# A Macaron block on one core: squarings of a matrix exponential against gates of three chunks moved among the expert tiles

## The chip, the cores and the metric

One core of one Trainium2 chip runs one launch. Times are device microseconds; of the kernel before there are three timed runs and one profiled execution. Five engines run side by side, each with a queue of its own that it works off in order: PE (TensorE), DVE (VectorE), ACT (ScalarE), POOL (GpSimd) and SP (SyncE, which only issues DMA here). They meet by semaphores. PEld is PE's weight load.

## The reference

`x` is 8 sequences of 512 rows of 128 floats. Three steps follow, each on a layer norm of what is there and each with a residual: half of a feed-forward, attention with 16 heads and a linear bias, half of a feed-forward again, with the same weights.

```python
xn = layernorm(x) * gamma + beta
abel_out = gelu(xn @ abel_w + abel_b)
logits = xn @ moe_gate_w + moe_gate_b
topw, topi = top_k(logits, 2)                 # of 8 experts
h = gelu(xn @ ew1[e] + eb1[e]);  eo = h @ ew2[e] + eb2[e]
moe_out = sum over the two experts of softmax(topw) * eo
for i in range(3): moe_out = moe_out @ expm(gens[i])
g = sigmoid(concat(abel_out, moe_out) @ gc_w + gc_b)
out = x + abel_out * (1 - g) + moe_out * g
```

## The kernel before, in words

Eight chunks (one sequence of 512 rows each) stay in SBUF as `x_all`. A feed-forward layer takes two steps.

**Gate of a chunk.** DVE takes statistics for two chunks at a time (`first_statistics`, lines 1414 to 1427), POOL the roots (`first_roots_`, L835), DVE a shift (`gate_shift`, L1628), ACT writes the normalised chunk twice (`z_`, L1140), PE turns it (`transpose_z`, L2197), ACT evacuates it (`xn_`, L1154), PE multiplies (`abel_logits`, L2213), ACT takes the Gelu (`abel_bias`, L1160), DVE finds the two best experts (`gate_top`), PE counts ranks (`ranks`), ACT takes the tanh of the gap, DVE works out the place of each row (`gate_place`, up to L1685), and POOL sends the rows with eight indirect DMAs of 128 rows to DRAM tensors `z_rows`, sorted by expert (`send_z`, L868).

**Expert tiles.** The sorted rows are worked off as 80 tiles of 128 rows: 20 quads of four tiles, 40 pairs of two. There are two runs: quads 0 to 5 (pairs 0 to 11) hold the rows of chunks 0 and 1 (`SPLIT[0] = 2`), quads 6 to 19 (pairs 12 to 39) those of chunks 2 to 7. Each run needs a table of its tiles (`count_rows`, `make_table`), zeros in the gaps between experts (`zero_gaps` on SP) and all its rows in DRAM (`rows_ready`). For each quad SP reads four registers and issues four loads (`load_x`, L715), PE turns them (`x_turn`, L2246), ACT evacuates. For each pair PE does `up` (L2271), ACT the Gelu (L1254), PE `down` (L2286, L2288), DVE the weighting (L1799); DVE also copies the experts' first weights (L1846). SP stores each quad's result in `y_rows` (`store_y`, L683). After the store of the last quad of a run POOL gathers the pairs of a chunk (`gather`, L885) and adds them into x (`sum_pairs`, `finish_x`, L895 to L908); then attention of that chunk can begin (`attention_stats`, L1408, in the first layer beside pair 22 for chunk 0 and 29 for chunk 1).

**The exponential.** The three 128 x 128 generators are scaled by their norms, put through a Taylor series of degree 11 (`transposed_generators`, `second_power`, `third_power`, three times `horner_step`) and squared 18 times. A round squares three matrices: PE computes square and transpose of each (`square`, L2125 and L2126), DVE copies them where the norm asks for it (`keep_squares`, L1555). The product is folded into the experts' second weights (`fold_rotation`), which the first expert tile needs, together with their transposes (`transpose_w2`, evacuated by ACT in `w2_out`).

**The order before** is written out by hand for each engine. Chunks 0 and 1 are gated ahead of the exponential's series; then six turns, for chunks 2 to 7, of one gate and three rounds of squarings; then `fold_rotation`; then the experts. PE's program of the turns is (from line 2331):

```python
for n in range(2, CH):
    if n + 1 < CH:
        transpose_z(n + 1)
    square(range(3 * n - 6, 3 * n - 5))
    ranks(n)
    square(range(3 * n - 5, 3 * n - 4))
    if n + 1 < CH:
        abel_logits(n + 1)
    square(range(3 * n - 4, 3 * n - 3))
    if n - 2 < E // 2:
        transpose_w2(n - 2)
```

DVE's and ACT's follow the same turns, POOL's is `send_z` for chunk after chunk with the roots between. SP's queue holds the stores of the Abel part (`keep_abel`), the copies of key rows for attention (`key_rows`, 512 KB for two heads), the zeros and the loads of x, in one order.

## Time and profile before

| | |
|---|---|
| timed runs | 789.38, 791.55, 793.94 us; median 791.55 |
| profiled execution, first to last instruction | 883.8 us (no other time is given for it) |
| instructions | 16149 |
| PE busy | 683.1 us, 77% of the span |
| DVE busy | 568.2 us, 64% |
| POOL busy | 485.6 us, 55% |
| ACT busy | 410.8 us, 46% |
| first expert tile of the first layer on PE | 149.06 us |

The profiled execution is 92 us longer than the median of the timed runs. Rows give a start and a duration in us from the first instruction; in brackets stands how long the engine was idle before, and what released it. "remote", "issue" and "another core or an unknown queue" are waits without a releaser in the trace. A matmul in fp32 shows as two records; PEclk is the granted clock as a share of 2.4 GHz.

### The profile page before, as it was taken

Reading aid. Unit: us, or ns where it says so; the run is one execution under the profiler, and the core shown is the slowest. Engines: PE = TensorE matmul, PEld = TensorE weight load, DVE = VectorE, ACT = ScalarE, POOL = GpSimd, SP = SyncE. Lnnn points to the kernel's source line nnn. Section 1 sums busy time; section 2 is a strip of 40 time slices with the busy share of each in tenths; the row PEclk is TensorE's granted clock in tenths of the full one; section 3 lists DMA queues with packets and bytes.
Section 4 is the critical chain, followed back from the end, with each engine's and each line's share of the span. In section 5 each row is a group of like instructions: output and inputs, shape, how many; then the busy total and the mean of one; then the engine's idle time right before and its main releaser. Section 6 shows DMA issues by size and latency. Waiting matters only on the chain.

```text
span 883.8 us, 16149 instructions
## 1 busy us (share of the span) xinstructions
PE 683.1 (77%) x4719; PEld 492.3 (56%) x4719; DVE 568.2 (64%) x1922; ACT 410.8 (46%) x931; POOL 485.6 (55%) x588
## 2 busy tenths in 40 slices
PE   1465667979897798997988979999997777838760
PEld 1355656979793354654646545455544466837750
DVE  3675545968767876876767767787673235745538
ACT  2243411545560265664545645556554655615530
POOL 2656554034512666576866768373645466566661
PEclk9968777988898899998999999999997999969985
DMA  8614544744348313023050240302201235233525
GB/s 242 205 48 117 132 123 115 183 112 105 94 113 192 110 31 98 18 65 87 2 130 21 49 103 1 98 17 55 61 13 53 85 78 167 75 93 84 175 96 154
DMA packets 89825, 84.04 MB, mean 95 GB/s; under 512 B 14561, under 2 KB 72556, under 8 KB 89580
## 3 DMA queue, kind: packets, MB, share of 16 engines
q1 hardware_dynamic: 74472, 57.51, 25.8%
q0 software_dynamic: 8800, 19.72, 7.5%
q10 hardware_dynamic: 6468, 5.79, 2.8%
q8 instruction: 40, 0.66, 0.3%
q14 instruction: 45, 0.37, 0.1%
HBM read 43.84 MB, written 31.13 MB: 85 GB/s over the span
## 4 chain that ended last, share of the span: by engine, by line
PE 46%; DVE 15%; another core or an unknown queue 11%; issue 7%; ACT 7%; SPq 5%; ACTq 3%; DMA 3%; POOL 1%; DVEq 0%; POOLq 0%
PE bank L2361 6%; PE bank L2271 6%; PE bank L2401 6%; PE bank L2286 6%; PE bank L2426 6%; SPq L595 4%; DVE mx_of L1923 3%; PE pair L2449 2%; PE bank L2363 2%; ACT beside_parts L1254 2%; DMA qT<-mT_zero 2%; PE pair L2213 2%; PE bank L2246 1%; ACT arena L1326 1%
## 5 line engine op out<-in xcount | busy, mean ns | idle before, releaser
L1326 ACT ACTIVATE arena<-bank 128x512 f32<-128x512 f32 x320 | 184.0, 599 | 175.2 <-PE bank L2401 147.1
L1923 DVE TENSOR_REDUCE mx_of<-bank 128x4 f32<-128x512 f32 x320 | 204.2, 684 | 81.9 <-PE bank L2361 42.9
L2401 PE MATMUL bank<-qT,kZ 128*128 128x512 f32 (+3 forms) x512 | 156.9, 377 | 19.2 <-ACT arena L1326 12.4
L975 POOL TENSOR_SCALAR_AFFINE_SELECT arena<-arena 128x256 f32<-128x256 f32 (+1 forms) x192 | 95.4, 521 | 123.9 <-ACT arena L1326 122.5
L2361 PE MATMUL bank<-kZ,qT 128*128 128x512 f32 x320 | 148.5, 481 | 15.7 <-DVE mx_of L1923 6.2
L2401 PEld LDWEIGHTS bank<-qT,kZ 128*128 128x128 f32 x512 | 95.7, 197 | 49.2 <-ACT arena L1326 24.1
L868 POOL DMA_INDIRECT z_rows<-beside_kZ,place x80 | 78.7, 984 | 51.5 <-DVE place L1685 29.8
L2361 PEld LDWEIGHTS bank<-kZ,qT 128*128 128x128 f32 x320 | 63.1, 200 | 70.7 <-issue 31.4
L885 POOL DMA_INDIRECT sums<-y_rows,y_place x56 | 54.4, 971 | 84.9 <-DMA y_rows<-arena 70.0
L2426 PE MATMUL bank<-arena,vA 128*9 128x512 f32 (+3 forms) x1024 | 92.4, 440 | 5.2 <-POOL arena L975 2.7
L1254 ACT ACTIVATE beside_parts<-bank,hidden_bias 128x128 f32<-128x128 f32 x160 | 45.5, 381 | 69.6 <-remote 44.0
L2286 PE MATMUL bank<-w_rot,beside_parts 128*128 x320 | 51.2, 297 | 31.7 <-ACT beside_parts L1254 29.0
L1254 ACT ACTIVATE arena<-bank,hidden_bias 128x128 f32<-128x128 f32 x160 | 45.5, 371 | 48.7 <-PE bank L2271 33.4
L1799 DVE TENSOR_SCALAR arena<-bank,arena 128x132 f32<-128x132 f32 x128 | 39.3, 348 | 44.3 <-remote 25.1
L944 POOL DMA_INDIRECT y_rows<-arena x48 | 49.3, 1026 | 31.8 <-DVE arena L1799 20.5
L2286 PEld LDWEIGHTS bank<-w_rot,beside_parts 128*128 128x128 f32 x320 | 43.9, 197 | 36.2 <-issue 35.3
L2286 PE MATMUL bank<-w_rot,arena 128*128 x320 | 50.4, 295 | 7.0 <-issue 5.2
L868 POOL DMA_INDIRECT z_rows<-w,place x48 | 47.0, 979 | 13.4 <-issue 13.4
L2271 PE MATMUL bank<-beside_parts,beside_qT 128*128 128x128 f32 x320 | 46.6, 286 | 8.3 <-issue 5.1
L2363 PE MATMUL bank<-fixed,ident_bf 128*128 128x512 bf16 x128 | 52.5, 410 | 0.0
L2271 PE MATMUL bank<-arena 128*128 128x128 f32 x320 | 47.0, 291 | 3.8 <-DVE arena L1846 2.2
L2286 PEld LDWEIGHTS bank<-w_rot,arena 128*128 128x128 f32 x320 | 44.6, 200 | 9.0 <-issue 8.2
(286 smaller groups left out, 1306.7 us busy)
## 6 DMA issues: line engine op xcount, KB each, us to landing
arena<-z_rows SPq DMA_DIRECT2D x128, 66.0 KB
qT<-parts SPq DMA_DIRECT2D x42, 128.0 KB
kZ<-parts SPq DMA_DIRECT2D x168, 32.0 KB
y_rows<-arena SPq DMA_DIRECT2D x20, 264.0 KB, 3.3
kZ<-bias_k_r SPq DMA_DIRECT2D x8, 512.0 KB
beside_kZ<-y_rows SPq DMA_DIRECT2D x7, 528.0 KB, 3.9
z_rows<-in_spare SPq DMA_DIRECT2D x4, 528.0 KB
z_rows<-in_spare SPq DMA_DIRECT2D x32, 66.0 KB
```

Of the source, the lines that this page charges most:

```text
L868: g_.indirect_dma_start(z_rows[run], bass.IndirectOffsetOnAxis(place[g % DEEP][:, k, t:t + 1], 0), zz(g)[:, k, t, :], None).then_inc(z_sen ...
L885: g_.indirect_dma_start(terms(0, c)[0][:, t, k, :], None, y_rows[run], bass.IndirectOffsetOnAxis(y_place[:, c, k, t:t + 1], 0)).then_inc(s ...
L975: g_.affine_select(out=cut, in_=cut, compare_op=ALU.is_ge, fill=0.0, base=0, pattern=[[0, 2], [0, blocks], [1, P]], channel_multiplier=-1) ...
L1254: a_(hidden_rows(layer, p)[:, i, j, :], ps_up[p % 2][:, P * n:P * (n + 1)], ACT.Gelu, bias=hidden_bias[:, j, bass.ds(e, 1)]).then_inc(hidd ...
L1326: a_(dst, src, ACT.Exp).then_inc(exp_ok.sem, 1)
L1923: v.tensor_reduce(mx_of[:, queries, :, t, keys], ps_a[n % NA][:, :].rearrange("p (q n) -> p q n", q=NQ), AX.X, ALU.max).then_inc(reduced.s ...
L2271: last = mm(into, tile(w1_e, j), tile(turned_x(layer, q), t), start=True, stop=True)
L2286: mm(into, hidden_rows(layer, p)[:, i, j, :], w2_rot[:, bass.ds(e, 1), j, :].rearrange("p a n -> p (a n)"), start=(j == 0), stop=False)
L2361: last = mm(into, qT[u][:, t, P * queries:P * (queries + 1)], heads, start=True, stop=(queries != keys))
L2363: last = mm(into, ident_bf[:, :], mask_qk[:, :].unsqueeze(1).to_broadcast([P, NQ, P]), start=False, stop=True)
L2401: return mm(outp, kZ[u][:, h, lo:lo + P], qT[u][:, t, lo:SEQ], start=start, stop=True, skip_group_check=(kind != "full"))
L2426: last = mm(ps_o[32 * q:32 * q + HD + 1, kb * P:SEQ], vA[u][:, kb, NG * q + t, :], pT[t % 2][:, q, PT_KB[kb]:PT_KB[kb] + n], start=(kb == ...
```

## The change

The exponential's series goes first on PE and DVE, with the gates of chunks 0 and 1 between its steps. Three turns (chunks 2 to 4) carry six rounds each. The gates of chunks 5 to 7 go among expert pairs 0 to 8, with other PSUM banks; x then has one bank instead of two in the first layer. The second run's table is made at pairs 8 and 9, its first x is turned at pair 12 after `down(11)`. The statistics of chunks 4 to 7 go into the first and third turn. POOL sends in halves around the roots. SP's queue is put in a new order, with the loads of the second run's first five quads in one block after `store_y(4)`. Nine small loads go from ACT's queue to SP's, and ACT starts with a Gelu on four columns of ones. `gather(1)` is split around the sums of chunk 0. Attention's steps beside the experts come one pair later, the bias loads of `load_bias` at pairs 8 and 9 instead of 4 and 6.

```diff
+ROTATED = tuple((3 * q, 3) for q in range(4)) + ((12, 2), (14, 2))
+GATED_FIRST = 5
+ROUNDS = 6
+AT_GAPS, AT_SECOND_RUN = 3, 4
...
+        def ps_x(layer, q):
+            return banks[2 + q % 2] if layer else banks[2]
...
         def ps_z(g):
-            return banks[4][:, :] if g < CH else banks[6]
+            return banks[4] if g <= GATED_FIRST else banks[3] if g < CH else banks[6]
...
+        def turns_at(layer, p):
+            if layer == 0 and p == second_run(layer) - 1:
+                return SWITCH[0]
+            q = p // 2 + 1
+            return q if (p or layer == 0) and p % 2 == 0 and q < QUADS and q != run_start(layer) else None
...
@@ SP @@
-            for g in range(1, 3):
-                keep_abel(g)
+            keep_abel(1)
             zero_gaps(0)
+            keep_abel(2)
             for g in range(2):
                 key_rows_of(g)
...
+            keep_abel(3)
             for q in range(X_TOP):
                 load_x(0, q)
...
+            keep_abel(4)
+            key_rows_of(2)
             sp.wait_ge(w2T_pe, 4)
             for q in range(X_TOP, X_BUFS):
                 load_x(0, q)
-            for g in range(5, CH - 1):
-                key_rows_of(g)
-            key_rows(sp, 0, 2 * (CH - 1), 2)
-            zero_gaps(1)
-            z_sent_up_to(sp, CH - 1)
-            key_rows(sp, 1, 0, NG)
-            for q in range(X_BUFS, QUADS):
-                store_y(q - X_BUFS)
-                load_x(0, q)
+            for q in range(QUADS - X_BUFS):
+                if GATED_FIRST + q < CH:
+                    keep_abel(GATED_FIRST + q)
+                if q == AT_GAPS:
+                    zero_gaps(1)
+                store_y(q)
+                if 1 <= q <= 3:
+                    key_rows_of(q + 2)
+                if X_BUFS + q < SWITCH[0] or q > AT_SECOND_RUN:
+                    load_x(0, X_BUFS + q)
+                if q == AT_SECOND_RUN:
+                    for n in range(max(X_BUFS, SWITCH[0]), X_BUFS + q + 1):
+                        load_x(0, n)
+                if q == AT_SECOND_RUN + 1:
+                    key_rows_of(CH - 2)
+                    key_rows(sp, 0, 2 * (CH - 1), 2)
+                    key_rows(sp, 1, 0, NG)
@@ POOL @@
             send_z(0)
+            send_z(1, (0,))
             first_roots_(2)
-            send_z(1)
+            send_z(1, (1,))
+            send_z(2)
+            send_z(3, (0,))
             first_roots_(3)
-            for g in range(2, CH):
+            send_z(3, (1,))
+            for g in range(4, CH):
                 send_z(g)
@@ ACT @@
+            act.wait_ge(v_ones, 2)
+            a_(th[:, :], vA[1][:, 0, 0:NT, HD], ACT.Gelu)
...
+                    if p == 0:
+                        abel_bias(GATED_FIRST)
+                        z_(CH - 1)
+                        tanh_gap(GATED_FIRST)
+                    if p == 1:
+                        xn_(GATED_FIRST + 1)
+                    if p == 3:
+                        abel_bias(GATED_FIRST + 1)
+                        tanh_gap(GATED_FIRST + 1)
...
-            for n in range(2, CH):
+            for n in range(2, GATED_FIRST):
                 abel_bias(n)
-                if n + 1 < CH:
-                    xn_(n + 1)
+                xn_(n + 1)
                 tanh_gap(n)
-                if n + 2 < CH:
-                    z_(n + 2)
-                if n - 2 < E // 2:
-                    w2_out(n - 2)
+                z_(n + 2)
+                for q in (2 * n - 4, 2 * n - 3):
+                    if q < E // 2:
+                        w2_out(q)
@@ DVE, the turns @@
+            for n in range(2, GATED_FIRST):
+                first = ROUNDS * (n - 2)
                 gate_logits(n)
                 gate_top(n)
+                keep_squares(range(first, first + 1))
                 gate_place(n)
...
+                keep_squares(range(first + 1, first + 2))
                 if n == 2:
+                    first_statistics(2)
+                if n == 3:
+                    make_table(0, TABLE_STAGES[0:1])
+                if n == 4:
+                    first_statistics(3)
+                    gate_shift(6)
+                    gate_shift(7)
+                keep_squares(range(first + 2, first + 3))
...
+                keep_squares(range(first + 3, first + 4))
+                if n == 2:
+                    gate_shift(4)
+                    gate_shift(5)
...
+                keep_squares(range(first + 4, first + 6))
@@ DVE, beside the experts @@
-                    if p == 1:
+                    for g in range(GATED_FIRST, CH):
+                        if p == 3 * (g - GATED_FIRST):
+                            gate_logits(g)
+                            gate_top(g)
+                        if p == 3 * (g - GATED_FIRST) + 2:
+                            gate_place(g)
+                    if p == 8:
                         count_rows(1)
-                        make_table(1)
+                        make_table(1, TABLE_STAGES[0:1])
+                    if p == 9:
+                        make_table(1, TABLE_STAGES[1:3])
@@ PE, experts @@
                 for p in range(PAIRS + 1):
+                    if p == second_run(layer):
+                        down(p - 1)
+                        x_turn(p // 2)
                     if p < PAIRS:
                         up(p)
@@ PE, the prologue @@
             turn_norms()
+            spread_norms()
+            transposed_generators()
             transpose_z(0)
+            second_power()
...
+            third_power()
             transpose_z(1)
+            horner_step(0)
             ranks(0)
             abel_logits(1)
+            horner_step(1)
+            horner_step(2)
             ranks(1)
             transpose_z(2)
             turn_exponential()
...
+            for n in range(2, GATED_FIRST):
+                first = ROUNDS * (n - 2)
+                transpose_z(n + 1)
+                square(range(first, first + 1))
                 ranks(n)
+                square(range(first + 1, first + 3))
+                abel_logits(n + 1)
+                square(range(first + 3, first + 4))
+                for q in (2 * n - 4, 2 * n - 3):
+                    if q < E // 2:
+                        transpose_w2(q)
+                if n == 4:
+                    transpose_b2()
+                square(range(first + 4, first + 6))
             fold_rotation()
@@ PE, beside the experts @@
+                    for g in range(GATED_FIRST, CH):
+                        first = 3 * (g - GATED_FIRST) + 1
+                        if p == first:
+                            ranks(g)
+                        if g + 1 < CH and p == first - 1:
+                            transpose_z(g + 1)
+                        if g + 1 < CH and p == first + 1:
+                            abel_logits(g + 1)
```

## Rows read from the trace of the kernel before

**Rows 1.** The page: span, and the chain by engine
```profile
span 883.8 us, 16149 instructions
...
PE 46%; DVE 15%; another core or an unknown queue 11%; issue 7%; ACT 7%; SPq 5%; ACTq 3%; DMA 3%; POOL 1%; DVEq 0%; POOLq 0%
```

**Rows 2.** Stages: busy us (instructions) of PE, PEld, DVE, ACT, POOL; PEclk, DMA, GB/s
```profile
61.00:139.00 78.00, 50.67 (x360) 46.63 (x358) 42.37 (x227) 23.02 (x54) 41.77 (x43) 0.76 0.49 120
149.10:179.20 30.10, 28.71 (x234) 27.27 (x235) 25.25 (x106) 18.12 (x54) 0.00 (x0) 0.94 0.63 144
179.20:214.80 35.60, 29.98 (x239) 29.12 (x237) 25.40 (x93) 17.52 (x55) 13.90 (x14) 0.86 0.46 108
```

**Rows 3.** The chain, 60 to 150 us, then pieces: start, us, what
```profile
by line: another core or an unknown queue 22.9%; issue 9.7%; DVE arena L1555 8.4%; PE bank L2126 8.1%; PE bank L2125 8.0%; PE bank L2143 5.6%; PE pair L2213 5.1%; DVE top_i L1648 3.6%; ACT beside_kZ L1140 3.5%; DVE top L1645 2.1%; DVE w_rot
...
110.28 8.41 another core or an unknown queue
...
192.40 5.21 issue
```

**Rows 4.** Timeline of the prologue: start, us, engine, operation [idle before <-releaser]
```profile
15.92 1.28 ACT L1140 ACT_TABLE_LOAD   x1 [11.86 <-issue]
...
24.37 0.16 DVE L1478 COPY arena<-bank 128x3 f32<-128x3 f32 x1 [9.78 <-PE bank L2082]
...
47.20 0.22 DVE L1628 SCALAR_TENSOR_TENSOR shift<-mv_g,rstd_g 128x4 f32<-128x4 f32 x2
...
61.02 0.39 PE L2125 MATMUL bank<-arena 128*128 128x128 f32 x2
```

**Rows 5.** The same: z of one chunk on ACT
```profile
65.31 3.19 ACT L1140 ACTIVATE beside_kZ<-x_all,shift,rstd_g 128x128 f32<-128x128 f32 x8 [2.72 <-DVE shift L1628]
```

**Rows 6.** The same: squaring on PE, two matrices at each clock
```profile
98.44 0.39 PE L2125 MATMUL bank<-arena 128*128 128x128 f32 x2
...
98.89 0.39 PE L2125 MATMUL bank<-arena 128*128 128x128 f32 x2
...
136.46 0.63 PE L2125 MATMUL bank<-arena 128*128 128x128 f32 x2
...
137.31 0.64 PE L2125 MATMUL bank<-arena 128*128 128x128 f32 x2
```

**Rows 7.** The same: one chunk's gate on DVE, first, squares between, last
```profile
60.79 0.19 DVE L1633 COPY logit<-pair 128x32 f32<-128x32 f32 x1 [2.38 <-PE pair L2214]
...
63.03 1.10 DVE L1555 COPY_PREDICATED arena<-arena,bank 128x256 f32<-128x256 uint32 x3
...
65.04 0.17 DVE L1685 CAST place<-place_of 128x8 int32<-128x8 f32 x1
```

**Rows 8.** The same, POOL: a scatter, then gathers and sums of chunk 0
```profile
140.43 0.97 POOL L868 DMA_INDIRECT z_rows<-beside_kZ,place  x1 [0.30 <-issue]
...
186.24 1.06 POOL L885 DMA_INDIRECT sums<-y_rows,y_place  x1 [38.07 <-DMA y_rows<-arena]
187.61 0.97 POOL L885 DMA_INDIRECT sums<-y_rows,y_place  x1 [0.30 <-issue]
...
197.91 1.30 POOL L895 TENSOR_TENSOR sums<-sums 128x528 f32<-128x528 f32 x1 [1.75 <-DMA sums<-y_rows,y_place]
...
211.41 0.19 POOL L903 TENSOR_SCALAR gate<-gate 128x4 f32<-128x4 f32 x1 [10.49 <-ACT gate L1181]
```

**Rows 9.** SP's queue: a store, four loads; the page: stores, last column landing
```profile
182.53 0.38 SPq L683 DMA_DIRECT2D y_rows<-arena  x1
183.42 1.88 SPq L715 DMA_DIRECT2D arena<-z_rows  x4
...
y_rows<-arena SPq DMA_DIRECT2D x20, 264.0 KB, 3.3
```

**Rows 10.** Timeline of DVE at the first attention statistics
```profile
214.79 0.87 DVE L1408 BATCH_NORM_STATS2 stat<-x_all 128x6 f32<-128x128 f32 x4 [1.16 <-POOL x_all L908]
```

More of the change, by code:

```diff
@@ L641, in _ @@
                 spare_rows(run)
+            with nc.allow_non_contiguous_dma("the first biases, one to a partition"):
+                for j in range(NJ):
+                    sp.dma_start(hidden_bias[:, j, :], eb1[:, P * j:P * (j + 1)].rearrange("e p -> p e")).then_inc(ld_bias, 16)
             def keep_abel(g):
@@ L918, in first_experts @@
             def first_experts():
-                for b in range(2):
-                    gather(b)
-                    if b:
-                        attention_roots(0)
-                    sum_pairs(0, b)
-                    finish_x(0, b)
+                gather(0)
+                gather(1, (0,))
+                sum_pairs(0, 0)
+                finish_x(0, 0)
+                gather(1, (1,))
+                attention_roots(0)
+                sum_pairs(0, 1)
+                finish_x(0, 1)
                 attention_roots(1)
@@ L1106, in _ @@
             act.dma_start(x_all[:, 2 * NT:, :], xv[:, 2 * NT:, :]).then_inc(ld_x[1], 16)
-            with nc.allow_non_contiguous_dma("the first biases, one to a partition"):
-                for j in range(NJ):
-                    act.dma_start(hidden_bias[:, j, :], eb1[:, P * j:P * (j + 1)].rearrange("e p -> p e")).then_inc(ld_bias, 16)
-            for dst, vec in ((C_QB, q_b), (C_KB, k_b)):
-                act.dma_start(cols[:, dst:dst + 1], vec.rearrange("(p a) -> p a", a=1)).then_inc(ld_w, 16)
-            act.dma_start(cols[:, C_GCB:C_GCB + 1], gc_b.partition_broadcast(P)).then_inc(ld_w, 16)
-            for dst, vec in ((R_VB, v_b), (R_OB, o_b), (R_G1, gc_w[0:D, 0]), (R_G2, gc_w[D:2 * D, 0])):
-                act.dma_start(rows[:, dst:dst + D], vec.partition_broadcast(P)).then_inc(ld_w, 16)
+            act.wait_ge(v_ones, 2)
+            a_(th[:, :], vA[1][:, 0, 0:NT, HD], ACT.Gelu)
             def keep_small():
@@ L2136, in fold_rotation @@
                 mm(banks[3][:, 2 * P:2 * P + ROW], b2_T, rot_x, start=True, stop=True).then_inc(rot_pe, 1)
[L2137 to L2139 removed]
+                for q, (first, n) in enumerate(ROTATED):
                     if q == 3:
                         pe.wait_ge(bias_parts, 1)
[L2142 to L2143 removed]
+                    if q == 4:
+                        wait(pe, xn_ok, GATED_FIRST)
+                        wait(pe, placed, GATED_FIRST - 1, 5)
+                    for i in range(first, first + n):
+                        last = mm(banks[q][:, ROW * (i - first):ROW * (i - first + 1)], w2_T[:, i // NJ, i % NJ, :], rot_x,
                                   start=True, stop=True)
@@ L2204, in abel_logits @@
                     wait(pe, abel_biased, g - 1)
+                    if g > GATED_FIRST:
+                        wait(pe, placed, g - 1, 5)
                 elif g >= CH:
@@ L2218, in ranks @@
                 wait(pe, routed, g)
-                if g < CH:
-                    if g:
-                        wait(pe, placed, g - 1, 5)
-                else:
+                if 0 < g < GATED_FIRST:
+                    wait(pe, placed, g - 1, 5)
+                elif g >= GATED_FIRST:
                     wait(pe, abel_biased, g)
```

155 lines of the change are left out of this document (72 added, 83 removed).

## The prediction

> **What bounds the kernel now.** I read the page first, for its span and its chain [rows 1]: 883.8 us, with 11% of the chain (97 us) put down to "another core or an unknown queue". There is one core, so these are waits for which the trace has no releaser. The timed runs have a median of 791.55 us, 92.25 us less than this span, and about as much as those waits. So I take most of them to belong to the profiled execution, and work every sum twice: as profiled, and with the unknown waits out.
>
> Next, the table by stage [rows 2]. It has the squarings (61 to 139) and the stretches from the first expert tile (149.1, called E below) to pair 12 (179.2) and on to the first attention statistics (214.8). PE is busy 51 of 78 us in the squarings, at a granted clock of 0.76, and 29 of 30 us in pairs 0 to 11. The prologue is a chain of small steps handed between DVE and PE; the experts are bound by PE, some 2.3 us a pair. Everything behind the experts is untouched, so the question is when the first expert stage ends.
>
> The chain [rows 3] gives the unknown waits: 22.9% of the 90 us from 60 to 150, 20.6 us, the longest 8.41 us; in the expert stage PE has one of 5.21 us in the middle of a pair, and there are more.
>
> **Up to the squarings: 11 us less as profiled, 8.6 without unknown waits.** Today DVE stands 9.78 us for the transpose that spreads the norms, because PE has it behind the first chunk's logits, and these wait for an ACT whose first activation comes at 15.92, behind its DMA issues [rows 4]. With the exponential first and nine small loads moved to SP's queue, this idle time goes. The two loads of hidden biases sit behind SP's weights and are needed only at E, the seven others 35 us later than they land; I cost them at nothing. The Gelu put first moves one table load of 1.28 us, like the one in that row, under the wait for statistics. One block of statistics (2.7 us) leaves the stretch too; three Horner steps (6.3 us) enter it. The shift of chunk 2 comes at 47.2 - 9.8 - 2.7 - 2.4 (the unknown wait at 40.7, [rows 3]) + 6.3 + 1 for new hand-overs = 39.6. Two chunks of z on ACT follow at 3.19 each [rows 5], then 0.8 for xn, 2.7 for logits and 0.6 for a transpose: first squaring near 50 against 61.
>
> **The squarings: 2 us less, 8.7 with unknown waits.** All 18 rounds of three matrices stay. On PE a matrix takes 0.45 us at 2.4 GHz and 0.85 at 1.2 GHz [rows 6], a round 1.35 or 2.55. Now: 78 - 20.6 = 57.4 us, less 3.5 for a table is 53.9, or 9.0 for each of six cycles of one gate and three rounds. A gate takes DVE 60.79 to 65.21, less 0.9 for copies of squares inside, so 3.5 us [rows 7]; rounds at 1.8 (the clock is mixed) fill the rest. After: three gates 10.8, 18 rounds 32.4, table 2.5 (a part hides beside rounds), and two statistics moved in, each 2.7 less the 1.35 of a round beside it: 2.7. Three waits are new. In the first cycle PE's second transpose of w2 needs ACT's copy of the first, which sits behind z of chunk 4, whose shift DVE gives only after the fourth round: 3.2 + 0.6 + 0.5 = 4.3 us in which all squaring stands. The same pair of transposes costs 0.7 a cycle later. In the last cycle DVE waits for POOL's roots between statistics and shift: 1.9. Sum 55.3, so 2.1 less than 57.4. Of 20.6 us of unknown waits I keep 14, as a quarter of the instructions leaves and four of eight 512 KB key loads move out. Folding, 10 us, stays. E comes 10.7 us sooner without unknown waits, 19.7 as profiled.
>
> **The start of the second run: 19 us later against E.** The tiles of pair 12 on hold rows of chunks 2 to 7, so they need chunk 7's rows in DRAM. Today these are out before E. After, chunk 5 is placed in pair 2, chunk 6 in 5, chunk 7 in 8. Pair 2 begins at E + 6.4 today; abel, z of chunk 7 and its tanh go between ACT's first pairs, 4 us, so chunk 5 is placed near E + 10. Each chunk is 8 scatters on POOL at 0.97 + 0.30 us [rows 8]; 24 take 30.5, longer than the 20 us between placements, so POOL is the bound: E + 40.5. Landing takes 1.75, by the wait behind the last gather. SP then reads registers and issues four loads (0.9 + 1.9 us, [rows 9]), and they land in some 2.3: E + 47.4. Transpose and evacuation follow: pair 12 at E + 49 against E + 30.2. Both gated steps on PE (2.4 us a chunk) and DVE's 3.5 fit into those 49. PE idles some 12 us, and as ACT and DVE have no other pair, nothing covers it.
>
> One rule speaks further against this. These scatters now run beside DVE's copies of w1, as the gathers of this stage do already: those take 0.97 us, the scatters of the prologue 0.97 too [rows 8]. The Trainium skill (SBUF — State Buffer, "SBUF: two separate sides") says that GpSimd cannot write descriptors while VectorE runs a two-port copy, such as an fp32 copy within SBUF. By the rule the 24 scatters would be longer still; the rows show no such thing.
>
> **The first attention statistics.** They wait for POOL's gathers of chunk 0, which wait for the store of quad 5 (today's first gather starts at 186.2, 38 us idle before it [rows 8]). SP now has that store behind five groups of loads that wait for chunk 7: E + 42.3 + 5 x 2.8 = 56.3, landed after 3.3 [rows 9] at 59.6. Then 8 gathers and 4 of chunk 1 (15.1), 1.75 landing, 3.0 for sums, 3.4 to finish (211.41 to 214.79): E + 82.9. Today DVE gets there at 214.79, E + 65.7 [rows 10]; the step comes one pair later now, which gives 2.1 back: 15 us more as profiled. But today's number holds unknown waits. Without them, gathers and sums end at 200.9 and the finish at 204.4, E + 55.3: then the loss is 25.5.
>
> **What costs nothing.** One PSUM bank for x instead of two: each transpose has two pairs of time. The stores of abel and the key rows in SP's loop wait for work already done when their turn comes, and load_bias is due only at the end. Attention's steps one pair later end inside the stage. If the late key rows (2.5 MB) ran up to the operands, they would cost 1 to 3 us.
>
> **Sum.** As profiled: -19.7 + 15 = -4.7. Without unknown waits: -10.7 + 25.5 = +14.8. If the 92.25 us of difference are all of the 97 unknown us, the timed runs keep one in twenty: +14. If they are shared with the chain's 7% of "issue" (62 us), four in ten are kept: +7. I take the middle, +10: 791.55 + 10 = 801.5 us, with a changed profile near 880, which would look like a small gain. Anything within 0.5% (4 us) is no difference that timing this kernel can tell.
>
> **Rivals.**
> **Faster.** The mechanism is the waits in the squarings: if they are in the timed runs as in the profile, each of the three turns moved out takes its 4 us with it (20.6 us over six cycles is 3.4 each), and the wait at pair 12 falls together with the 5.21 us that stood at 192.4. Then -19.7 + 15, and down to -8 if rounds go at 1.35 us because PE idles less: 783 to 788. It decides once E is more than 20 us sooner in timed runs. For it: waits of up to 8.41 us stand in this stretch. Against: 92 us have to go somewhere. 0.16.
> **No difference.** E gains 16 to 20 and the stage loses as much, or the chunk-5 placement comes at E + 7 and the store of quad 5 is not last: 788 to 795. 0.19.
> **Much slower.** PE comes back from 12 us idle, and from the stop before the statistics, at 1.2 GHz: the window with the stop at 192.4 has a mean clock of 0.86, the one before it 0.94. If scatters of chunk 4 are late too (POOL waits for the roots of chunks 6 and 7 with half of chunk 3 unsent), POOL's 30.8 us begin later by up to 10: 812 to 822. 0.08. The Trainium skill (TensorE: Matmul & The Clock Gate, "What's actually happening") has the clock halved by default and released by activity, which is this cost; the trace agrees.
> **The change does not do what it says:** the squarings end where they do now (139) because 18 rounds are the chain whatever stands between; E gains only the 11 us before them. The result is then the forecast's upper side, 805 to 812, and is held within it.
>
> **Chances.** The forecast, 795.5 to 812, has 0.57. Leaving out some 0.1 below and above gives 785 to 815. Bounds of single terms: the first gains 7 to 12, the squarings -6 to +14 in gain, pair 12 loses 14 to 23 (placement between E + 6 and E + 13), the statistics 10 to 27. Faster 0.16, same 0.19, slower 0.65.
>
> **What would show it.** First squaring near 50; a stop of about 4 us in the first cycle, all engines but ACT idle, ACT in z of chunk 4; first expert tile near 130; POOL in unbroken scatters from E + 10 to E + 40.5; PE idle over 10 us before pair 12, released by the loads from z_rows; DVE idle at the statistics in pair 23, released by POOL's x_all. I am wrong if pair 12 begins before E + 40, or if E is before 120.

## Result and the profile after

The changed kernel takes 806.82 us (median of 4, 803.48 to 809.98), the kernel before beside it 790.46 us (median of 4, 787.67 to 793.94): ratio 1.0207, 95% interval 1.0164 to 1.0250, so slower by 16.4 us. The prediction had 801.5 us, 785 to 815, and slower as the likeliest case.

The profile of before on which the prediction was built spans 883.8 us [rows 1]. The same kernel was profiled once more, unchanged. First lines of the page and the chain by engine, the second execution of the kernel before:

```profile
span 791.0 us, 16149 instructions
...
PE 49%; DVE 20%; DMA 7%; issue 7%; POOL 5%; ACT 4%; ACTq 3%; SPq 3%; DVEq 0%; POOLq 0%
```

and of the changed kernel:

```profile
span 807.5 us, 16155 instructions
...
PE 38%; DVE 20%; issue 11%; POOL 10%; DMA 9%; ACT 5%; SPq 4%; ACTq 1%; DVEq 0%; POOLq 0%
```

The entry "another core or an unknown queue" (11% in [rows 1]) is in neither. What has grown is POOL's share of the chain, from 5 to 10%, and "issue", from 7 to 11%; PE's has fallen from 49 to 38%, with the same 656 us of busy time. From here on "before" is this second execution, and the two spans differ by 16.5 us, which is the timed difference.

E is the first transpose of an expert tile. The marks of before: first squaring, E, pair 12, first attention statistics, first score matmul:

```profile
58.92 0.64 PE L2125 MATMUL bank<-arena 128*128 128x128 f32 x2
...
117.87 1.09 PE L2246 MATMUL bank<-ident,arena 128*128 128x128 f32 x8 [0.69 <-DVEq L1403]
...
147.23 1.00 PE L2271 MATMUL bank<-arena 128*128 128x128 f32 x7
...
174.84 0.86 DVE L1408 BATCH_NORM_STATS2 stat<-x_all 128x6 f32<-128x128 f32 x4
...
226.36 0.71 PE L2361 MATMUL bank<-kZ,qT 128*128 128x512 f32 x2 [0.80 <-DVE arena L1799]
```

The same marks of the changed kernel, with the transpose ahead of pair 12:

```profile
51.37 0.63 PE L2206 MATMUL bank<-arena 128*128 128x128 f32 x2
...
110.33 0.63 PE L2332 MATMUL bank<-ident,arena 128*128 128x128 f32 x4 [1.30 <-DVEq L1448]
...
160.32 0.90 PE L2332 MATMUL bank<-ident,arena 128*128 128x128 f32 x3 [9.06 <-DMA arena<-z_rows]
162.31 2.08 PE L2357 MATMUL bank<-arena 128*128 128x128 f32 x8 [0.87 <-ACT arena L1281]
...
196.07 0.87 DVE L1453 BATCH_NORM_STATS2 stat<-x_all 128x6 f32<-128x128 f32 x4 [2.28 <-POOL x_all L942]
...
243.67 0.73 PE L2450 MATMUL bank<-kZ,qT 128*128 128x512 f32 x2 [1.03 <-DMA kZ<-oT]
```

Subtracting gives the account; "predicted" is the column of the prediction's sum without unknown waits:

| | before | after | difference | predicted |
|---|---|---|---|---|
| start to first squaring | 58.9 | 51.4 | -7.5 | -8.6 |
| first squaring to E | 58.95 | 58.96 | 0.0 | -2.1 |
| E to pair 12 | 29.4 | 52.0 | +22.6 | +18.8 |
| E to first statistics | 57.0 | 85.7 | +28.7 | +27.6 |
| E to first score matmul | 108.5 | 133.3 | +24.8 | +25.5 |
| score matmul to the end | 564.6 | 563.8 | -0.8 | 0 |

The sum is -7.5 + 0 + 24.8 - 0.8 = +16.5.

The stage by windows, before (E to pair 12); columns as in [rows 2]:

```profile
117.90:147.20 29.30, 27.22 (x234) 25.92 (x235) 25.45 (x106) 17.98 (x54) 8.02 (x6) 1.00 0.84 193
```

and after, with the stop ahead of pair 12 as a row of its own:

```profile
110.30:151.30 41.00, 32.73 (x296) 30.73 (x296) 32.24 (x171) 23.74 (x70) 25.00 (x26) 1.00 0.55 142
151.30:162.30 11.00, 1.12 (x4) 0.72 (x4) 2.35 (x14) 0.78 (x1) 2.93 (x1) 0.55 0.48 117
```

Twelve pairs take 41 us instead of 29, with gates between them (PE busy 32.7 us of 41, 27.2 of 29), and then hardly any engine works for 11 us (PE 1.1 us of them, POOL 2.9). What ends the stop, POOL and SP of the changed kernel:

```profile
120.07 1.01 POOL L902 DMA_INDIRECT z_rows<-beside_kZ,place  x1 [8.97 <-DVE place L1738]
...
150.31 0.97 POOL L902 DMA_INDIRECT z_rows<-beside_kZ,place  x1 [0.30 <-issue]
...
148.45 0.50 SPq L629 DMA_DIRECT2D kZ<-bias_k_r  x1
149.71 0.36 SPq L713 DMA_DIRECT2D y_rows<-arena  x1
156.90 11.84 SPq L745 DMA_DIRECT2D arena<-z_rows  x20
168.79 0.42 SPq L713 DMA_DIRECT2D y_rows<-arena  x1
```

Chunk 5's first scatter is at E + 9.7, the last of the 24 at E + 40.0, with its end at E + 41.0. The first row of SP is a load of key rows, 512 KB. SP issues its first load 5.6 us after that scatter's end; its waits in this stretch name the landing of the scatters:

```profile
SPq L535 <- DMA z_rows<-beside_kZ,place: 6.0, 1, 6.0
```

In the squarings the two new stops stand where the prediction put them:

```profile
65.28 1.11 PE L2193 MATMUL bank<-ident,arena 128*128 128x128 f32 x4 [3.85 <-ACT arena L1156]
...
96.25 0.49 PE L2206 MATMUL bank<-arena 128*128 128x128 f32 x2 [2.71 <-DVE arena L1609]
```

The first is the second transpose of w2 behind z of chunk 4. The second is PE waiting for squares while DVE waits for POOL's roots.

### The profile page after: what moved, and what is told of

Same layout as the page of the kernel before. It is cut to its first block, busy times and chain, and to the rows that moved or that the text cites. A ratio compares the mean times of both kernels' runs of the same rounds, so it can differ in the third digit from the quotient of the medians.

```text
span 807.5 us, 16155 instructions
## 1 busy us (share of the span) xinstructions
PE 655.5 (81%) x4719; PEld 473.3 (59%) x4719; DVE 563.6 (70%) x1922; ACT 410.1 (51%) x931; POOL 488.7 (61%) x588
## 4 chain that ended last, share of the span: by engine, by line
PE 38%; DVE 20%; issue 11%; POOL 10%; DMA 9%; ACT 5%; SPq 4%; ACTq 1%; DVEq 0%; POOLq 0%
PE bank L2515 7%; PE bank L2450 7%; PE bank L2490 6%; POOL z_rows L902 5%; DVE mx_of L1996 4%; DMA qT<-mT_zero 3%; POOL y_rows L980 3%; PE bank L2357 2%; PE bank L2452 2%; PE bank L2372 2%; SPq L617 2%; PE pair L2297 2%; PE pair L2538 2%; DVE arena L1852 1%; SPq L745 1%
## 5 line engine op out<-in xcount | busy, mean ns | idle before, releaser
L2490 PE MATMUL bank<-qT,kZ 128*128 128x512 f32 (+3 forms) x512 | 154.4, 371 | 5.7 <-DMA qT<-mT_zero 4.7
L2450 PE MATMUL bank<-kZ,qT 128*128 128x512 f32 x320 | 145.9, 470 | 14.9 <-DVE mx_of L1996 5.4
L2490 PEld LDWEIGHTS bank<-qT,kZ 128*128 128x128 f32 x512 | 93.6, 192 | 33.7 <-ACT arena L1371 14.1
L902 POOL DMA_INDIRECT z_rows<-beside_kZ,place x80 | 80.5, 1006 | 38.1 <-issue 22.4
L2450 PEld LDWEIGHTS bank<-kZ,qT 128*128 128x128 f32 x320 | 61.1, 193 | 71.4 <-DVE mx_of L1996 34.9
L2372 PE MATMUL bank<-w_rot,arena 128*128 x320 | 48.3, 287 | 3.8 <-ACT arena L1302 2.9
L2372 PE MATMUL bank<-w_rot,beside_parts 128*128 x320 | 48.5, 288 | 1.6 <-ACT beside_parts L1302 1.6
L2357 PEld LDWEIGHTS bank<-arena 128*128 128x128 f32 x320 | 41.2, 201 | 11.2 <-issue 7.2
L2357 PE MATMUL bank<-beside_parts,beside_qT 128*128 128x128 f32 x320 | 44.2, 281 | 3.6 <-DVE beside_qT L1899 1.9
L2372 PEld LDWEIGHTS bank<-w_rot,arena 128*128 128x128 f32 x320 | 42.6, 192 | 6.0 <-issue 5.4
```

Of the source, the lines that this page charges most:

```text
L902: g_.indirect_dma_start(z_rows[run], bass.IndirectOffsetOnAxis(place[g % DEEP][:, k, t:t + 1], 0), zz(g)[:, k, t, :], None).then_inc(z_sen ...
L2357: last = mm(into, tile(w1_e, j), tile(turned_x(layer, q), t), start=True, stop=True)
L2372: mm(into, hidden_rows(layer, p)[:, i, j, :], w2_rot[:, bass.ds(e, 1), j, :].rearrange("p a n -> p (a n)"), start=(j == 0), stop=False)
L2450: last = mm(into, qT[u][:, t, P * queries:P * (queries + 1)], heads, start=True, stop=(queries != keys))
L2490: return mm(outp, kZ[u][:, h, lo:lo + P], qT[u][:, t, lo:SEQ], start=start, stop=True, skip_group_check=(kind != "full"))
```

## The experiments

All times but the first are medians, each with the ratio to the kernel before timed beside it, and in brackets that ratio's 95% interval.

**The kernel before, once more.** No edit.

> The kernel before, unchanged, profiled once more. The first profile of it spanned 883.8 us beside timed runs of 791.6. My theory (the unknown waits belong to that one execution): this span is near 791, the chain has no share of another core or an unknown queue, the first expert tile (E) starts near 149.1 - 30 = 119 us, the squarings take 57.4 us, and the first score matmul comes near E + 106, against E + 133.3 in the changed kernel: the loss of the change then lies wholly between E and that matmul (27 us) and the prologue gives 7 to 10 back. The rival (the waits are a property of the kernel, and the changed one has fewer of them): the span is again above 850, with waits that have no releaser in the squarings.

Measured: one time of 792.76 us, span 791.0, no unknown waits, E at 117.9, squarings 51.2 us (to the folding's second product; 50.4 to the first, where the window of [rows 2] ends, and 57.4 expected), first score matmul at E + 108.5. The first theory holds: the 92 us belonged to one profiled execution, and the timed runs show none of them.

**The exponential alone.** All eight gates stay ahead of the experts, three rounds to a turn.

```diff
+            largest_norms()
             gate_shift(0)
             gate_shift(1)
-            gate_bias_rows()
-            largest_norms()
+            norms_of_all()
+            scale_generators()
...
+            horner_step(2)
+            gate_place(1)
...
             turn_exponential()
+            first_statistics(2)
+            first_statistics(3)
             for n in range(2, CH):
```

> The kernel before with the first half of the change alone: matrix exponential, its transposes and the first squares ahead of the logits, the nine small loads on SP's queue, the Gelu first. All eight gates stay ahead of the experts, in turns of three rounds. My theory (the prologue's part is a gain, the move of the gates the loss): first squaring near 51 instead of 61 to 59, E 7 to 10 us sooner, nothing behind E changed, so 782 to 785 us, ratio to before 0.988 to 0.992. Rival 1 (the move of the small loads and the Gelu delay SP's or ACT's later work as much as the exponential gains): 790, no difference. Rival 2 (the squarings' new order is what costs): first squaring near 51 but E not sooner, 790.

Measured: 781.63 us, 0.9896 (0.9851 to 0.9942). First squaring and E:

```profile
49.94 0.63 PE L2139 MATMUL bank<-arena 128*128 128x128 f32 x2
...
108.38 1.07 PE L2260 MATMUL bank<-ident,arena 128*128 128x128 f32 x8 [1.43 <-DVEq L1405]
```

E is 9.5 us sooner than before, and the first score matmul comes at E + 106.7 (108.5 before). The exponential's part of the change is a gain of 7.5 us (781.63 against 789.12 beside it). All the rest of the change, the moved gates with everything that came with them, then costs some 25 us (ratio 1.0207 / 0.9896 = 1.031). One thing in that rest is that this kernel keeps the statistics ahead of the turns, where the changed one has them between rounds. With six gates in the squarings, E is still 2 us sooner than in the changed kernel with three.

**The store of quad 5 ahead of the block of loads.**

```diff
-AT_GAPS, AT_SECOND_RUN = 3, 4
+AT_GAPS, AT_SECOND_RUN = 3, 5
```

(and, one time, DVE's output of a pair ahead of its w1 copies.)

> The changed kernel with one thing moved: SP issues the store of quad 5 ahead of the loads of quads 6 to 11 instead of behind five of them. This is my term for the first attention statistics (store landed at E + 59.6 predicted, at E + 63.8 measured). Theory A (the stage's loss is the wait for chunk 7's rows at pair 12, and the statistics' late gathers are hidden under pairs 12 to 22): pair 12 stays at E + 52, the gathers start 15 to 20 us sooner, DVE's idle time of 2.3 us at the statistics goes, and the time falls by 2 to 3 us, to 804. Theory B (the late store is a loss of its own, the 10 us by which the statistics are later than pair 12 was late): 795 to 798.

Measured: 803.84 us, 1.0167 (1.0119 to 1.0215). The transpose ahead of pair 12 comes at E + 51.4 (E + 50.0 in the changed kernel), as SP's loads now stand behind one more store. The gathers start at E + 50.2 instead of E + 63.8, and DVE's stop at the statistics is gone:

```profile
160.34 1.06 POOL L919 DMA_INDIRECT sums<-y_rows,y_place  x1 [5.61 <-DMA y_rows<-arena]
...
192.93 0.86 DVE L1453 BATCH_NORM_STATS2 stat<-x_all 128x6 f32<-128x128 f32 x4
```

Theory A: gathers 13.6 us sooner, with pair 12 a little later, give some 3 us. The intervals of the two ratios overlap, so that 3 is no more than the medians say; theory B's 795 to 798 lies below all six runs (800.23 to 806.54).

**Three chunks in the first run.** Four more pairs between E and the first tile that needs chunk 7.

```diff
-SPLIT = (2, 6)
+SPLIT = (3, 6)
-AT_GAPS, AT_SECOND_RUN = 3, 4
+AT_GAPS, AT_SECOND_RUN = 3, 7
```

(and, here and in the next run, DVE's output of a pair ahead of its w1 copies once, as in the run above.)

> The changed kernel with three chunks instead of two in the first run of sorted rows (8 quads, 16 pairs), so that four more pairs stand between E and the first tile that needs chunk 7's rows; the same sums. Chunk 2's rows take the place in the first run, and POOL's 24 scatters are the same. Theory A (the loss is that POOL's scatters outlast the pairs before the second run): the stop ahead of the second run, 11 us and more at pair 12, shrinks to 1 to 4 us ahead of pair 16, and the time falls by 7 to 11 us, to 796 to 800. Theory B (the loss is in POOL's and SP's queues as such, gathers and stores behind them, wherever the second run starts): the stop shrinks, but the first statistics stay near E + 85 with an idle time of 7 us or more on PE there, and the time stays within 3 us of the changed kernel's, 804 to 808.

Measured: 800.92 us, 1.0120 (1.0072 to 1.0169), just above theory A's 796 to 800 and below theory B's 804 to 808. The stop only shrank, to 6.7 us, and SP was why: four stores in a row kept it until 162.8, 14 us after the last scatter's end (issued at 147.6; the expectation of the next run has 149.5, which is wrong).

```profile
148.17 14.64 SPq L713 DMA_DIRECT2D y_rows<-arena  x4
...
167.40 0.90 PE L2335 MATMUL bank<-ident,arena 128*128 128x128 f32 x3 [6.72 <-DMA arena<-z_rows]
```

**The same with the loads ahead of the store of quad 7.**

```diff
-AT_GAPS, AT_SECOND_RUN = 3, 7
+AT_GAPS, AT_SECOND_RUN = 3, 6
```

> The kernel with three chunks in the first run once more, with SP's block of loads of the second run ahead of the store of quad 7 instead of behind it. In the run before this one SP stood until 163 in stores that waited for DVE, though POOL's last scatter was issued at 149.5, and PE stood 6.7 us ahead of pair 16. Theory A (POOL's scatters, and behind them SP's order, set the start of the second run): the loads start near E + 47 instead of E + 56.6, PE's stop ahead of pair 16 is at most 2 us, and the time is 5 to 7 us less than with the store first: 794 to 796. Theory B (the pairs before, at 3.4 us each with the gates between them, are what is slow, and loads are only just in time): the stop goes but pairs stretch, 799 to 801.

Measured: 810.07 us, 1.0256 (1.0221 to 1.0292): both theories wrong, 9 us slower than with the store first (11 by the ratios). The stop ahead of pair 16 halved, but the loads began only at E + 53.4 (the store of quad 6 stood ahead), quad 7's store went out behind 20 of them, and chunk 0's gathers need it:

```profile
162.79 11.46 SPq L745 DMA_DIRECT2D arena<-z_rows  x20
174.30 0.42 SPq L713 DMA_DIRECT2D y_rows<-arena  x1
...
166.28 0.66 PE L2335 MATMUL bank<-ident,arena 128*128 128x128 f32 x4 [3.18 <-DMA arena<-z_rows]
...
178.72 1.06 POOL L919 DMA_INDIRECT sums<-y_rows,y_place  x1 [24.86 <-DMA y_rows<-arena]
...
199.53 0.68 DVE L1453 BATCH_NORM_STATS2 stat<-x_all 128x6 f32<-128x128 f32 x3 [11.87 <-POOL x_all L942]
```

In one queue, with one wait in it for the last chunk, either the second run or the first sums come late.

**Statistics early.** The two statistics go into DVE's idle time ahead of chunk 2's logits.

```diff
             turn_exponential()
+            first_statistics(2)
+            first_statistics(3)
             for n in range(2, GATED_FIRST):
...
                 keep_squares(range(first, first + 1))
+                if n == 2:
+                    gate_shift(4)
+                    gate_shift(5)
+                if n == 4:
+                    gate_shift(6)
+                    gate_shift(7)
```

(with the same calls further down taken out.)

> The changed kernel with the third and fourth block of first statistics moved ahead of chunk 2's logits, where DVE stands idle for 5.9 us, and with the shifts of chunks 4 and 5 one round, and of 6 and 7 two rounds, sooner. My theory (the moved gates gain nothing ahead of E because new waits take it back: 3.85 us for ACT behind z of chunk 4, 2.7 us for POOL's roots, 5.3 us of statistics between rounds): both stops go, squarings shrink from 52 to 42 to 45 us, E comes 7 to 9 us sooner at 101 to 103, and as the scatters after E move with it, the time falls by 6 to 9 us, to 798 to 801. Rival (the rounds of squarings themselves are the chain, at whichever clock, and hide what stands between): E within 3 us of 110, the time 804 to 807.

Measured: 797.26 us, 1.0104 (1.0071 to 1.0137), 9.6 us less than the changed kernel (8 by the ratios; 6 to 9 expected). E, and the two transposes of w2 with 0.69 us between them where 3.85 stood:

```profile
62.42 0.66 PE L2192 MATMUL bank<-ident,arena 128*128 128x128 f32 x4 [0.69 <-ACT arena L1156]
...
101.56 0.66 PE L2331 MATMUL bank<-ident,arena 128*128 128x128 f32 x4 [0.58 <-DVEq L1448]
```

First squaring (52.11) to E is 49.5 us, against 59.0 in the changed kernel and in before, and 58.4 with the exponential alone. PE has no stop of over 1.5 us left in this stretch, and its granted clock there is 0.94 (0.90 in the changed kernel). So three gates moved out are worth 9 us, some 3 each, and the change as made spent all of it. The stop at pair 12 stands: 8.4 us ahead of the transpose at E + 49.3.

**More work on POOL.** Eight multiplications ahead of chunk 7's scatters, into a buffer whose content nobody reads.

```diff
+                if g == CH - 1:
+                    wait(pool, placed, g)
+                    z_done(pool, g)
+                    for i in range(8):
+                        g_.tensor_tensor(v_next..., zz(g)..., zz(g)..., ALU.mult).then_inc(extra, 1)
+                        pool.wait_ge(extra, i + 1)
                 send_z(g)
```

> The changed kernel with eight multiplications of 128x512 on POOL, into a buffer that is not yet in use, ahead of the scatters of chunk 7: some 11 us more work on POOL, nothing else. If POOL's scatters set the start of the second run, pair 12 comes 10 to 12 us later (E + 62 to 64), PE's and ACT's stops grow by as much, and the time is 816 to 819. If SP, landing or the pairs' own pace set it, the time rises by less than 4 us, to 807 to 811.

Measured: 812.71 us, 1.0280 (1.0233 to 1.0327), 5.9 us more, between the two. The addition took 9.36 us, the last scatter came 9.8 us later against E, SP's first load and the transpose ahead of pair 12 only 6.0 and 6.1 later:

```profile
141.15 9.36 POOL L1088 TENSOR_TENSOR v_next<-beside_kZ 128x512 f32<-128x512 f32 x8
...
159.83 0.95 POOL L903 DMA_INDIRECT z_rows<-beside_kZ,place  x1 [0.31 <-DMA y_rows<-arena]
...
162.69 1.41 SPq L746 DMA_DIRECT2D arena<-z_rows  x3
...
166.15 1.11 PE L2340 MATMUL bank<-ident,arena 128*128 128x128 f32 x4 [7.47 <-DMA arena<-z_rows]
```

From the last scatter's end to SP's load it is 1.9 us here, 5.6 in the changed kernel. The DMA packets say where the 5.6 come from. q0 carries the scatters, q1 what SP issues; a row gives packets, MB and the time of the packets as a share of all 16 DMA engines. First the changed kernel from 148.6 to 153.0, right behind SP's load of key rows at 148.45, then this kernel from 158.0 to 161.8, where the same load, issued at 149.91, is long done:

```profile
q1 hardware_dynamic: 756, 0.69, 79.2%
q0 software_dynamic: 36, 0.08, 6.6%
...
q1 hardware_dynamic: 445, 0.23, 18.7%
q0 software_dynamic: 97, 0.20, 16.1%
```

A scatter is 32 packets (768 for the 24). In the changed kernel the last three (96 packets) moved 36 by 153.0 and the other 60 by 155.8, while just before that load, from 144.8 to 148.6, four scatters of the same unbroken row moved their 128. So it is not the length of the row that makes the last ones late, but what SP has put into the DMA engines beside them. In four kernels the last scatter ends 2.2, 2.8, 4.0 and 10.9 us behind the issue of that load (key loads late, changed, early statistics, this one), and SP's first load follows it by 5.5, 5.6, 4.8 and 1.9 us. This is read from the traces: no run moved that load alone.

Pair 12's transpose is 6.1 us later and the first score matmul 7.6, both against E; the time is 5.9 us longer, of which the two intervals leave 1 to 11. The rest of the 9.8 us was covered by the shorter lag.

**One gate among the pairs.** Five in the squarings, with 4, 4, 4, 3 and 3 rounds; loads of the second run behind the store of quad 2.

```diff
-GATED_FIRST = 5
-ROUNDS = 6
-AT_GAPS, AT_SECOND_RUN = 3, 4
+GATED_FIRST = 7
+ROUNDS_AT = (0, 4, 8, 12, 15, 18)
+AT_GAPS, AT_SECOND_RUN = 1, 2
```

(and what follows from it on each engine: statistics early, scatters again in whole chunks, one w2 transpose to a turn, key rows of chunks 3 to 5 earlier on SP, the second run's table at pairs 3 and 4.)

> The changed kernel with only the last chunk's gate among the pairs (five gates in the squarings, with 4, 4, 4, 3 and 3 rounds), statistics early, and SP's loads of the second run behind the store of quad 2. After E, POOL has the rest of chunk 6 and 8 scatters of chunk 7 instead of 24 and more. My theory (a gate moved is free as long as its scatters, their landing and the loads fit ahead of pair 12): the last scatter is issued near E + 20, loads start near E + 26, no stop at pair 12 (under 2 us), E at 103 to 106, and the time is 775 to 781, below the kernel before by 9 to 14 us. Rival (any gate among the pairs stretches the pairs on PE, ACT and DVE, or pair 12 comes late even for one chunk, as SP's loads stand behind a wait): a stop of 4 us and more at pair 12, 784 to 792.

Measured: 791.88 us, 1.0040 (1.0020 to 1.0060). E at 106.14, and pair 12 at E + 32.8 with no stop, as my theory had it; but not the time, which is the rival's 784 to 792. The loss had moved to the gathers and the statistics:

```profile
140.26 1.45 SPq L629 DMA_DIRECT2D kZ<-bias_k_r  x3
141.75 1.50 SPq L713 DMA_DIRECT2D y_rows<-arena  x1
143.77 5.88 SPq L745 DMA_DIRECT2D arena<-z_rows  x4
149.70 0.53 SPq L713 DMA_DIRECT2D y_rows<-arena  x1
...
157.17 1.06 POOL L923 DMA_INDIRECT sums<-y_rows,y_place  x1 [29.48 <-DMA y_rows<-arena]
...
178.28 0.87 DVE L1442 BATCH_NORM_STATS2 stat<-x_all 128x6 f32<-128x128 f32 x4 [8.85 <-POOL x_all L946]
```

**The same with the key loads moved.** One goes to between the stores of quads 1 and 2, two behind the store of quad 11.

```diff
-                if q == AT_SECOND_RUN + 1:
+                if q == 1:
                     key_rows_of(CH - 2)
+                if q == 11:
                     key_rows(sp, 0, 2 * (CH - 1), 2)
                     key_rows(sp, 1, 0, NG)
```

> The kernel with one gate among the pairs, with two of its three late key loads (1.5 MB of the three) moved from behind the load of quad 9 to behind the store of quad 11, and the third ahead of the second store. In its trace the second run came in time (pair 12 at E + 32.8), but POOL's first gather came at E + 51.0, against E + 36.6 in the kernel before, behind a store of quad 5 that SP issued at E + 43.6, and DVE then stood 8.85 us at the first statistics. Theory A (the key loads crowd the second run's loads and the stores behind them, so the gathers are late): the store of quad 5 goes out near E + 38, the gather starts near E + 42, DVE's stop is under 2 us, and the time falls by 8 to 10 us, to 781 to 784. Theory B (the wait for chunk 7's rows on SP, ahead of three stores, is what is late, whatever the key loads do): the gather stays later than E + 47 and the time above 787.

Measured: 783.26 us, 0.9913 (0.9885 to 0.9942), 8.6 us less (10 by the ratios). Theory A, but for the size of what is left: the store of quad 5 goes out at E + 36.6, the gathers start at E + 42.1, and DVE's stop is 5.6 us, not under 2.

```profile
144.21 0.43 SPq L713 DMA_DIRECT2D y_rows<-arena  x1
...
149.74 1.06 POOL L924 DMA_INDIRECT sums<-y_rows,y_place  x1 [21.82 <-DMA y_rows<-arena]
...
171.56 0.68 DVE L1443 BATCH_NORM_STATS2 stat<-x_all 128x6 f32<-128x128 f32 x3 [5.59 <-POOL x_all L947]
```

**The key loads moved in the kernel with early statistics**, all three behind the store of quad 11.

> The changed kernel with early statistics (797.3) and its three late key loads moved behind the store of quad 11 too. I priced the late key rows at 1 to 3 us in the prediction and left them out of the sum. In the trace PE stood 5.2 us at 182.6 for rows of a quad whose load SP issued behind them. Theory A (the key loads cost what they crowd): that stop goes and the time is 792 to 795. Theory B (they are hidden, and the stores and loads are late because they stand in one queue behind chunk 7's rows): 796 to 798.

Measured: 797.09 us, 1.0084 (1.0052 to 1.0115), no change clear of the intervals: theory B. PE's stop of 5.2 us at 182.6 went, one of 3.3 at 184.1 came. The first gather is at 164.99 against 164.94: here the store of quad 5 stood ahead of the key loads already. With one gate it stood behind them.

## Why the prediction was right, and where it was off

**The sum.** The side was right, and so was the main mechanism, a second run that waits for POOL's scatters; the size was off above all because of one step: "I take the middle, +10". The two sums were built for an unknown share of unknown waits, and the prediction kept between one in twenty and four in ten of them. The clean execution keeps none, and the sum without them was +14.8 against a measured +16.4. That this comes so near is in part luck. Its +25.5 was taken at the first attention statistics, over the late gathers, which turned out not to be what holds the stage; by the predicted terms up to pair 12 alone it is -10.7 + 18.8 = +8.1, and squarings that gained nothing and a pair 12 that lost 3.8 more made up the rest. The difference between the two times given for before (883.8 and 791.55) said as much: the unknown waits in the page (97 us) explained it whole.

One sign that the prediction gave of being wrong came true: "if E is before 120". E is at 110.3, where "near 130" was forecast. Both numbers were made from the 149.06 of the long profile. In the clean one E is at 117.9 before the change, so the sign says nothing about the change; but it says that the levels of the long profile could not be used. Taking the unknown waits out did not mend them either: first squaring to E is 88.0 us there, 67.4 less the 20.6 of unknown waits, and 58.95 in the clean execution. PE was also busy longer in the long one, at a lower granted clock (50.67 us at 0.76 in [rows 2], 42.12 us at 0.91 from 58.9 to 110.1 in the clean one), for the same work.

**Up to the squarings** (-8.6): -7.5, first squaring at 51.4 ("near 50").

**The squarings** (-2.1): nothing gained. The two named waits came close to their price, 3.85 (4.3) and 2.71 on PE (1.9). The levels were both too long: 50.4 us from the first squaring to the folding's first product before, where I had 57.4, and 51.4 after, where I had 55.3. Rounds with nothing between them go at 1.35 us at full clock (82.47 to 85.15 are two), not at 1.8. What the sum lacked is the clock after the new stops. Behind the two stops nine matrices ran at the slow level of [rows 6] (windows 66 to 81 and 96 to 103.7, granted clock 0.85 and 0.78), 0.4 us each, 3.6 in all; before, three did, behind a stop of 4.1 us. (The three gates were also put in at 10.8 us, where 3.5 each is 10.5.) The result is that of the rival "the change does not do what it says" (E gains only what lies before the squarings, 805 to 812), but not for its reason: the rounds are not the chain, as early statistics took 9.5 us out of the same stretch. The 3.5 us for a gate [rows 7] was near right; the statistics between rounds, the two stops and the clock behind them ate it.

**The start of the second run** (+18.8): +22.6. Placement at E + 9.7 ("near E + 10") and the last scatter at E + 40.0 to 41.0 ("E + 40.5") are right. The mis-sized term is the landing. From the last scatter's end to SP's first load the sum had 2.65 us (1.75 by the row behind a gather [rows 8], and 0.9 for the registers); it was 5.6. The extra 3 us fall together with SP's load of key rows at 148.45, of the kind that the prediction priced at nothing because it waits for work already done: it waited for nothing, but its packets had the DMA engines. The 2.3 us for the landing of SP's loads has no row before; from the end of the fourth one's issue to the transpose it was 1.5 after. And pair 12 came at E + 29.4 before, not E + 30.2. The window without work is 11.0 us, PE's own idle time in it 9.06 ("some 12"). That POOL's scatters bound pair 12 is shown by the added work, 6.1 of whose 9.8 us came through; that four more pairs help only as far as SP's order lets them is shown by the two runs with three chunks.

The sentence on the scatters beside w1 copies: of the 24, seventeen took 0.97 us and the longest 1.48, as the rows of before had it, and one of 0.97 (at 125.21) has w1 copies at 125.23 and 125.99 beside it. The rule of the Trainium skill (SBUF — State Buffer, "SBUF: two separate sides") that would have made them longer is not seen in this case.

**The first attention statistics** (E + 82.9): E + 85.7, against 57.0 today (55.3). Right as a time, but it is not a loss of its own: with the store moved, gathers 13.6 us sooner gave 3 us. It follows pair 12, and takes over when pair 12 is cured (one gate) or when the gathers are made later still (three chunks, loads first).

**What costs nothing.** The three last loads of key rows were nothing here, and 8.6 us in the kernel with one gate: the price depends on which store stands behind them. The one ahead of the second run's loads is the one with the late scatters. That one PSUM bank for x is enough was not tried by itself.

**Rivals.** "Faster" and "no difference" both needed unknown waits in the timed runs. "Much slower" had the clock after the stop: PE ran at a granted clock of 0.50 for 3.7 us behind it, at 1.00 afterwards: some 1.9 us lost, an estimate (half of the 3.7), where that case needed some 10. The trace agrees with what the prediction cites from the Trainium skill (TensorE: Matmul & The Clock Gate, "What's actually happening"): halved after the stop, released by work.

```profile
162.30:166.00 3.70, 3.69 (x17) 3.69 (x18) 1.47 (x7) 1.48 (x5) 0.00 (x0) 0.50 0.46 109
166.00:170.00 4.00, 4.00 (x38) 3.94 (x38) 3.68 (x12) 2.78 (x10) 0.00 (x0) 1.00 0.51 129
```

**Which version to keep.** The exponential first with all gates ahead of the experts (0.9896, 0.9851 to 0.9942), or with one gate among the pairs and the key loads moved (0.9913, 0.9885 to 0.9942). Both beat both kernels; the runs don't rank them. The first is the smaller edit. Whether the 5.6 us left at the second one's statistics can be had was not tried.

**Open.** Whether SP's load of chunk 5's key rows, put behind the second run's loads, gives back the 3 us at pair 12 was not tried. Why twelve pairs with gates between them take 41 us and not 29 was only read from the trace (stops of 2.0, 1.65 and 2.79 us, for ACT once and for DVE's w1 copies twice), not taken apart by a run.

## What to carry to other kernels

When a profile is longer than the timed runs by as much as its waits without a releaser, take those waits out of every term, price nothing by them, and if you can, profile it once more before you take any level from it. A step moved off one chain takes its whole tail along, here 24 scatters, their landing and the loads behind them: count instructions times pitch on the engine that issues them, and compare with the work that is left in front of the first reader. Look also at what large loads other queues have in flight when the last of that tail must land. And before a gain is booked for taking work out of an alternating chain of two engines, look at what is put into it in the same edit; here two statistics between rounds and a pair of transposes behind a late shift cost what three gates had given.

## What the runs showed of the hardware that was not expected

- How late scatters land depends on what other queues move at that time. From the last one's end to the first load that waits for it: 5.6 us with a 512 KB load of SP's issued 2.8 us before that end, 1.9 us with it issued 10.9 us before. In the first case the scatters' packets had 6.6% of the DMA engines' time and SP's 79%.
- One profiled execution of the same kernel spanned 883.8 us and the next 791.0, with timed runs near 790 throughout. The extra time stood mostly in waits without a releaser: 20.6 us of them from 60 to 150, and over half of the 97 us behind 600.
- Three loads of 512 KB on SP's queue, ahead of four loads of 66 KB, stretched the issue of those four from 1.88 us to 5.88.
